# A scan's output projection from f16 halves with a factor per chunk, in another place of the step

## The chip, the cores and the metric

One core of a Trainium2 chip runs the whole program. The metric is device time in microseconds (us). "Before" is the kernel as it stands, "after" the one with the change. The engines are named as the profile does: PE (TensorE matmuls), PEld (its weight loads), DVE (VectorE), ACT (ScalarE), POOL (GpSimd), SP (SyncE, which here only issues DMAs).

## The reference, cut to what matters

```
x   = x + 0.5 * ffn(layernorm(x))            # quantised weight, LoRA, bias; 2048 tokens x 512
n   = layernorm(x)
h   = n' + mamba2(rmsnorm(n))                # residual of the block is the layer-normed input
        zxbcdt = h @ w_in.T                  # z 512, x 128, B 128, C 512, dt 4
        causal convolution with 4 taps, silu; dt = softplus(dt + bias)
        scan over 16 chunks of 128 tokens, 4 heads of 128: Y from att * X and from the state
        y = (Y + D x) * silu(z)              # 2048 x 512
        return y @ w_out.T                   # 512 x 512: the product that is changed
h2  = rmsnorm(h);  mlp = (silu(h2 @ gate.T) * (h2 @ up.T)) @ down.T      # inner size 1792
x   = x + h + mlp
x   = x + 0.5 * ffn(layernorm(x))
```

## The kernel before, in words

Tokens are worked in 16 chunks `c` of 128 and in 4 strips `i` of 512 (`c = 4i + j`). Nearly all large products are made of f16 halves: a value is scaled, ACT writes its f16 rounding ("hi"), DVE the f16 of the rest ("lo"), and the helper `product` (its matmul is L1960) sums hi*hi, hi*lo and lo*hi for each of four 128-row blocks, so 12 matmuls of 512 columns for one product of 128 x 512 x 512. A few products are still in f32; the profile shows each f32 matmul as two records.

The middle of the program is `step(c)` for c = 0 to 15, written once for each engine as a fixed order of work, which is all the order there is: every engine runs its own list and waits on semaphores.

- TensorE's step: `s1(c+1)` (decay rows and transposes of the next chunk), `f(c+8)` (first ffn of a later chunk, while there is one), `s2_diag`, `s2_state`, `s2_inner` (the scan proper; `s2_diag(c)` and `s2_state(c)` sum into the bank `B_YT`), `s1_bc(c+1)`, one `proj` of the next strip (a product, the first of `SLOTS[j]`), with j = 0 also `steps` and with j = 2 `csm`, then `w(c)` (the output projection, L2083: four f32 matmuls of `szs` with `w_out`), then the remaining one or two `proj` of `SLOTS[j][1:]`. In the last strip (c = 12 to 15) two products `gate_up(0, j)` stand in place of the `proj`.
- `steps(i)` makes the four step-size columns of each chunk of a strip with `product`: 48 matmuls of 4 columns. `csm(i)` sums them along the tokens.
- DVE's step: tap sums of the convolution for the late `proj` of the step before (`taps`, L1450, after ACT has copied the bank out with `conv`, L885), `x1_stats(c+8)` (L1382, L1289), `gate_y(c)` (Y times silu(z), L1425, ends the use of `B_YT`), `lo2(c-1)` (the lo half of h2, L1376), `advance(c)` (the state, L1432), `weights` and `scan1(c+1)` (L1415, on which POOL's `scan_d` and then `s2_diag(c+1)` wait), `lo1`, `prep0`, the taps of the first slot, `residual2(c)` (L1441: n1 plus the bank of `w(c)`).
- ACT's step: `scan_ecs`, `scan1`, `conv` and tanh of the late slots, `hi0`, `hi2(c-1)`, `scan_decay(c+1)`, `hi1`, `scan2(c+1)`, `renorm(c)` (n1, L799), `conv` and tanh of the first slot, `square(c)` (sum of squares of the residual, L803).
- POOL's step: the rsqrt and shift of ln1 and ln0, `scan_c`, `scan_d`, the DMA `xb`, `rms2(c)` (from `square(c)`; it then issues the DMA that adds x2 into xs), and in some steps the sums `t_op` for the later Strassen products.
- SP issues the loads of x, the transposes `t0`, `t1(c+8)` and `t2(c-1)` (h2 into `h2`), one queue in order.

Banks of the `proj`, `f` and `w` products are handed out by a list (`PLAN`) that is built in the order of TensorE's step. `w_out` is loaded whole in f32 early on, and its memory later becomes one of the three homes of the gated values. After step 15 come the mlp products and the second ffn, which the change touches only by their first waits.

## Times and profile before

| what | value |
|---|---|
| median of 3 runs | 767.16 us (766.51 to 767.99) |
| the profiled execution, its own time | 768.65 us |
| its span on the core | 766.9 us |
| PE busy | 755.4 us, 98% |
| DVE busy | 626.5 us, 82% |
| ACT busy | 446.4 us, 58% |
| POOL busy | 337.2 us, 44% |
| granted TensorE clock | 9 tenths or more in all 40 slices, 1.00 in every window read |

The page gives the busy time of each engine, then the span in 40 slices, then the chain of work that ended last, then groups of instructions. PE is busy in nearly the whole span, so a time can be found by adding up PE's list, provided that no other engine keeps PE waiting; the waits and the windows say how near the others are to doing so. Matmul durations in the rows overlap each other, so the cost of a group is read from start to start, or in the chain, which counts no overlap.

### The profile page before, as it was taken

The page shows a single profiled execution, that of the slowest core. Times are in us where ns is not written, and L with a number is a line of the kernel's source. Part 1 is how long each engine was busy: PE and PEld are TensorE (multiplying, and loading weights), DVE is VectorE, ACT ScalarE, POOL GpSimd, SP SyncE. Part 2 cuts the span into 40 slices and gives each one's busy share as a digit, 9 for nine tenths or more (in the row PEclk, how much of TensorE's full clock was granted, in tenths as well). Part 3 has the DMA queues.
Part 4 walks back from the last instruction along what each step waited for, and adds up shares of the span by engine and source line. Part 5 has one row for each costly group of instructions (what it writes and reads, how often), then busy time and mean ns, then how long its engine had stood idle before and what let it go on. Part 6 is the DMA issues. An engine that isn't in the chain of part 4 may idle for free.

```text
span 766.9 us, 10654 instructions
## 1 busy us (share of the span) xinstructions
PE 755.4 (98%) x3469; PEld 353.2 (46%) x3470; DVE 626.5 (82%) x1230; ACT 446.4 (58%) x881; POOL 337.2 (44%) x392
## 2 busy tenths in 40 slices
PE   8999999999999999999999999999999999999998
PEld 3444554454555444444443444444444444444443
DVE  6888878878878979878799978878878878767994
ACT  3877767766686766643545556456456456444441
POOL 5631534663442379775413333233233233224574
PEclk9999999999999999999999999999999999999999
DMA  8843543552321211420521743743743743443565
GB/s 311 171 75 71 139 94 83 110 111 60 78 56 28 42 38 42 114 55 1 124 47 23 172 77 64 163 77 62 164 77 65 162 77 66 79 77 69 119 169 138
DMA packets 95414, 71.86 MB, mean 94 GB/s; under 512 B 65232, under 2 KB 72400, under 8 KB 95360
## 3 DMA queue, kind: packets, MB, share of 16 engines
q0 software_dynamic: 17280, 31.46, 23.0%
q1 hardware_dynamic: 77600, 39.66, 19.5%
q8 instruction: 28, 0.46, 0.2%
q14 instruction: 26, 0.21, 0.1%
q10 hardware_dynamic: 480, 0.07, 0.1%
HBM read 20.32 MB, written 4.19 MB: 32 GB/s over the span
## 4 chain that ended last, share of the span: by engine, by line
PE 77%; DVE 13%; ACT 4%; issue 3%; POOL 2%; DMA 1%; ACTq 0%; POOLq 0%; DVEq 0%
PE PS L1960 64%; PE PS L2083 4%; PE PS L2183 3%; DVE raw L1450 2%; PE PS L2091 1%; DVE stage L1450 1%; PE PS L2056 1%; DVE state L1432 1%; PE PS L2065 1%; DVE st L1289 1%; PE PS L2073 1%; PE PS L2048 1%; DVE xs L1382 1%; DVE S L1415 1%; DMA h<-lora_b_t 1%
## 5 line engine op out<-in xcount | busy, mean ns | idle before, releaser
L712 POOL DMA_DIRECT2D xs<-x x59 | 50.9, 864 | 151.2 <-ACT x L1159 137.1
L1960 PE MATMUL PS<-h,w_in 128*128 128x512 f16 x480 | 108.7, 379 | 0.2 <-issue 0.2
L1960 PE MATMUL PS<-h,x_t 128*128 128x512 f16 x408 | 94.0, 379 | 0.0
L1960 PEld LDWEIGHTS PS<-h,w_in 128*128 128x128 f16 x480 | 46.9, 98 | 65.3 <-issue 15.5
L1960 PE MATMUL PS<-n_T,stage 128*128 128x512 f16 x288 | 71.5, 379 | 0.0
L1159 ACT ACTIVATE x<-PS,d_d 128x512 f32<-128x512 f32 x59 | 40.2, 682 | 39.1 <-PE PS L1960 39.1
L1960 PEld LDWEIGHTS PS<-h,x_t 128*128 128x128 f16 x408 | 39.5, 98 | 48.5 <-issue 2.3
L521 POOL TENSOR_TENSOR r<-mv,mhalf 128x1 f32<-128x1 f32 (+1 forms) x32 | 29.4, 917 | 72.2 <-DVE mv L1293 55.0
L712 POOL DMA_DIRECT2D xs<-n x29 | 25.2, 868 | 71.1 <-ACT n L1159 60.8
L1960 PE MATMUL PS<-pre,stage 128*128 128x512 f16 x192 | 49.3, 379 | 0.0
L1129 ACT ACTIVATE xds<-tm,dgh 128x512 f32<-128x512 f32 x24 | 17.3, 722 | 53.0 <-DVE tm L1889 53.0
L1960 PEld LDWEIGHTS PS<-n_T,stage 128*128 128x128 f16 x288 | 28.1, 98 | 34.0 <-ACT x L1159 0.3
L1960 PE MATMUL PS<-w_ffn,raw_gu 128*128 128x512 f16 x192 | 43.2, 379 | 0.0
L1450 DVE SCALAR_TENSOR_TENSOR raw<-pre,cw,raw 128x512 f32<-128x512 f32 x36 | 28.0, 777 | 10.4 <-ACT raw L885 10.1
L1960 PE MATMUL PS<-raw,x_t 128*128 128x512 f16 x144 | 34.7, 379 | 0.4 <-DVE Ld L1842 0.4
L1960 PE MATMUL PS<-w_in,x_t 128*128 128x512 f16 x144 | 34.8, 379 | 0.0
L1159 ACT ACTIVATE n<-PS,d_d 128x512 f32<-128x512 f32 x29 | 19.8, 683 | 23.8 <-PE PS L1960 22.5
L1960 PE MATMUL PS<-h,n 128*128 128x512 f16 x144 | 33.2, 379 | 0.3 <-DVE n L1530 0.3
L2083 PE MATMUL PS<-w_out,stage 128*128 128x512 f32 x64 | 29.3, 600 | 0.3 <-DVE stage L1425 0.2
L1960 PEld LDWEIGHTS PS<-pre,stage 128*128 128x128 f16 x192 | 18.7, 98 | 22.7 <-ACT x L1159 0.3
L1960 PEld LDWEIGHTS PS<-w_ffn,raw_gu 128*128 128x128 f16 x192 | 18.7, 98 | 22.7 <-DMA raw_gu<-h2n_p 0.3
L2083 PE MATMUL PS<-w_out,raw 128*128 128x512 f32 x64 | 29.0, 595 | 0.1
(314 smaller groups left out, 1819.3 us busy)
## 6 DMA issues: line engine op xcount, KB each, us to landing
xs<-x POOLq DMA_DIRECT2D x75, 256.0 KB, 3.3
xs<-n POOLq DMA_DIRECT2D x29, 256.0 KB, 3.3
x_t<-x_in SPq DMA_DIRECT2D x16, 256.0 KB, 3.0
x_t<-hb POOLq DMA_DIRECT2D x16, 256.0 KB, 3.8
out<-x_t SPq DMA_DIRECT2D x16, 256.0 KB, 2.3
raw_gu<-gate_t SPq DMA_DIRECT2D x7, 512.0 KB, 4.4
raw_gu<-up_t SPq DMA_DIRECT2D x7, 512.0 KB, 6.6
raw_d<-down_t SPq DMA_DIRECT2D x7, 512.0 KB, 7.3
```

Source lines behind the costliest of these rows:

```text
L521: return po.tensor_tensor(dst, src, mhalf[:, 0:src.shape[-1]], ALU.pow)
L712: po.dma_start(chunk_of(xs, c), d_tmps[d % 3], accum_op=ALU.add).then_inc(s_acc[d % 3], 16)
L1129: ac.activation(th_s[ab], u4 if ab else c11, ACT.Tanh, scale=dgh[:, p % 2:p % 2 + 1]).then_inc(e_tanh_g, 1)
L1159: ac.activation(d_tmps[d % 3], bank(d_bank(d)), ACT.Copy, scale=d_d[:, p % 3:p % 3 + 1]).then_inc(e_ev, 1)
L1289: link(ve.bn_stats(stat, src), e_link, base + 1)
L1382: link(ve.scalar_tensor_tensor(chunk_of(xs, c), bank(b), 0.5 / ACT_SCALE if c < NF else d_f[:, :], x_t[:, j, :], ALU.mult, ALU.add), e_x1, ...
L1415: last = ve.scalar_tensor_tensor(S[:, s, h, :], heads(B_G)[:, h, :], dt[:, (c // CH) % 2, j * H + h:j * H + h + 1], Ld[:, h, :], ALU.mult, ...
L1432: last = ve.scalar_tensor_tensor(state[:, h, :], state[:, h, :], ecs[:, s, h, P - 1:P], heads(B_SS)[:, h, :], ALU.mult, ALU.add)
L1450: ins = ve.scalar_tensor_tensor(xbc[i % 2][:, b, :], pre[:, w, k:k + ST], cw[:, b, k:k + 1], xbc[i % 2][:, b, :], ALU.mult, ALU.add)
L1960: ins = pe.matmul(out_, lhs(a, b, k), rhs(a, b, k), start=first and n == 0, stop=last and n == len(todo) - 1)
L2083: last = pe.matmul(bank(b), y[:, h, (c % CH) * P:(c % CH + 1) * P], w_out[:, h, :], start=h == 0, stop=h == H - 1)
L2183: last = pe.matmul(bank(B_P[c % 2]), nT32[c % 2][:, k, :], wf[:, k, :], start=k == 0, stop=k == KB - 1)
```

## The change

- `w(c)` becomes a `product`: 12 f16 matmuls instead of four f32 ones. `w_out` is cut once, in the prologue, into f16 halves with a power-of-two scale per row (`wo_sum`, `wo_hi` on ACT, `wo_scale`, `wo_lo` on DVE). Its f32 load goes to a part of `h2` that held the quantised weight (`wo_raw`), is issued after the small loads and waits for the ffn weight (`e_wf`).
- y is cut in every chunk, with a factor for the chunk: ACT sums its squares (`y_sum`), TensorE adds them over the partitions with one f32 matmul of one column into `B_YT` (`y_over`), DVE takes it with a floor (`y_max`), POOL takes the powers -1/2 and 1/2 (`y_scale`), ACT writes hi (`y_hi`), DVE lo (`y_lo`). `residual2` multiplies the bank with the factor back.
- `w(c-1)` stands in step c, ahead of the first `proj`, and `w(15)` after `gate_up(0, 4)` in the bank `B_CS`. With it `residual2`, `renorm`, `square` go from c to c-1, and `hi2`, `lo2`, `rms2`, `t2` from c-1 to c-2 (`rms2` to the head of POOL's step). `csm` stands ahead of the `proj`, `bound_turn(0)` behind `s1_bc`. Four `t_op` of c = 14 go behind the last step, around `rms2(15)`.
- `s2_diag(c)` waits for `y_max(c-1)` instead of `gate_y(c-1)`.
- `steps` uses hi and lo weights side by side in eight columns (`w_dt`): 32 matmuls instead of 48, one small DVE add more.
- Several one-off semaphores give way to the engines' own counters (same waits).

```diff
-        w_out = sb("w_out", [P, H, DM])
+        w_out = sb("w_out", [P, 2, H, DM], F16)
-            sp_.dma_start(w_out[:, :, :], w_out_t...).then_inc(s_wout, 16)
+            sp_.wait_ge(e_wf, KB)
+            sp_.dma_start(wo_raw, w_out_t...).then_inc(s_wout, 16)
...
+            def y_scale(c):
+                po.wait_ge(e_ym, c + 2)
+                po.tensor_tensor(y_s[:, c, :], y_m[:, c, :], halves[:, :], ALU.pow).then_inc(e_yscale, 1)
...
             def step(c):                     # POOL
+                if c > 1:
+                    rms2(c - 2, c % CH)
                 ...
                     scan_d(c + 1, (c + 1) % CH)
+                y_scale(c)
...
+            def y_sum(c):
+                ac.wait_ge(e_y, c + 1)
+                ac.activation(junk..., y_of(c), ACT.Square, accum_out=ssy[:, c:c + 1]).then_inc(e_ysum, 1)
+            def y_hi(c):
+                ac.wait_ge(e_yscale, c + 1)
+                if c > 0:
+                    ac.wait_ge(e_wo, c)
+                ac.activation(y_hl[:, 0, :, :], y_of(c), ACT.Copy, scale=y_s[:, c, 0:1]).then_inc(e_yhi, 1)
...
+            def y_max(c):
+                ve.wait_ge(e_yall, c + 1)
+                ve.tensor_scalar(y_m[:, c, :], PS[:, B_YT, 0:1].broadcast_to([P, 2]), Y_TINY, None, ALU.max).then_inc(e_ym, 1)
+            def y_lo(c):
+                ve.wait_ge(e_yhi, c + 2)
+                ve.scalar_tensor_tensor(y_hl[:, 1, :, :], szs[(c // CH) % 2][:, :, cols], y_s[:, c, 0:1], y_hl[:, 0, :, :],
+                                        ALU.mult, ALU.subtract).then_inc(e_ylo, 1)
...
-                ve.tensor_tensor(x2[:, j % 2, :], n1[:, :], bank(PLAN["w", c][0]), ALU.add).then_inc(e_x2, 1)
+                ve.scalar_tensor_tensor(x2[:, j % 2, :], bank(PLAN["w", c][0]), y_s[:, c, 1:2], n1[:, :], ALU.mult, ALU.add)...
...
             def w(c):
-                for h in range(H):
-                    last = pe.matmul(bank(b), y[:, h, ...], w_out[:, h, :], start=h == 0, stop=h == H - 1)
+                pe.wait_ge(e_ylo, H + c + 1)
+                pe.wait_ge(*freed)
+                product(bank(b), lambda a, b, h: y_hl[:, a, h, :], lambda a, b, h: w_out[:, b, h, :], H).then_inc(e_wo, 1)
+            def y_over(c):
+                pe.wait_ge(e_ysum, c + 2)
                 pe.wait_ge(e_y, c + 1)
+                pe.matmul(PS[:, B_YT, 0:1], ssy[:, c:c + 1].broadcast_to([P, P]), over[:, :], start=True, stop=True).then_inc(e_yall, 1)
...
             def s2_diag(c, j):
-                    pe.wait_ge(e_y, c)
+                    pe.wait_ge(e_ym, c + 1)
...
             def step(c):                     # TensorE
                 ...
                     s1_bc(c + 1)
+                if c > 0:
+                    w(c - 1)
+                if j == 2 and i + 1 < NS:
+                    csm(i + 1)
                 if i + 1 < NS:
                     proj(i + 1, SLOTS[j][0])
                     if j == 0:
                         steps(i + 1)
                 else:
                     gate_up(0, j)
-                w(c)
                 if i + 1 < NS:
-                    for q in SLOTS[j][1:]:
+                    for n, q in enumerate(SLOTS[j][1:]):
                         proj(i + 1, q)
+                        if n == 0:
+                            y_over(c)
...
             gate_up(0, EARLY_GU)
+            w(NCH - 1)
             bound_spread(1)
```

In the last strip `y_over(c)` stands between the two products of `gate_up(0, j)`.

## Rows read from the trace of the kernel before

**Rows 1.** Page, part 1: busy us, share of the span, instructions.

```profile
PE 755.4 (98%) x3469; PEld 353.2 (46%) x3470; DVE 626.5 (82%) x1230; ACT 446.4 (58%) x881; POOL 337.2 (44%) x392
```

**Rows 2.** Waits of PE, whole span: waiting line <- line waited for: us, times, longest.

```profile
PE PS L2056 <- POOL S L555: 1.0, 1, 1.0
```

**Rows 3.** Windows, from s1 to s1: length, busy (count) PE, PEld, DVE, ACT, POOL, clock, DMA.

```profile
106.40:174.60 68.20, 67.93 (x334) 33.87 (x333) 56.52 (x140) 49.16 (x111) 35.71 (x44) 1.00 0.42 88
174.60:240.00 65.40, 65.24 (x321) 32.67 (x320) 53.33 (x123) 47.90 (x113) 27.21 (x34) 1.00 0.29 60
240.00:296.40 56.40, 54.57 (x229) 26.97 (x227) 47.39 (x108) 39.48 (x93) 30.97 (x31) 1.00 0.19 38
296.40:338.30 41.90, 41.88 (x174) 20.35 (x172) 37.47 (x60) 21.50 (x48) 33.17 (x32) 1.00 0.35 82
```

**Rows 4.** Chain that ended last, in order of time: start, us, what.

```profile
97.83 3.54 PE PS L2083 x8
...
122.42 0.70 DVE raw L1450
...
227.70 3.78 PE PS L1960 x60
...
305.66 3.43 PE PS L2083 x8
...
390.17 2.59 PE PS L1960 x12
392.76 0.31 PE PS L2129 x2
```

**Rows 5.** Timeline of PE about 121 and 199 us: start, us, instructions.

```profile
121.88 0.39 PE L2037 MATMUL PS<-cs_b,sel_b 80*128 80x128 bf16 x4
...
130.98 0.29 PE L2012 MATMUL PS<-dA,tri 128*128 128x16 f32 x2
131.12 0.42 PE L2013 MATMUL PS<-tri,dA 128*80 128x128 f32 x2
```

**Rows 6.** Timelines of DVE and (the L549 row) POOL: start, us, instructions.

```profile
119.24 0.68 DVE L1364 TENSOR_TENSOR hn_p<-hn,hn_p 128x512 f16<-128x512 f32 x1
...
133.20 0.74 DVE L1376 SCALAR_TENSOR_TENSOR h2n_p<-x,r,h2n_p 128x512 f16<-128x512 f32 x1
...
340.51 0.15 DVE L1497 COPY mxa<-PS 128x3 f32<-128x3 f32 x1
...
115.62 1.56 DVE L1376 SCALAR_TENSOR_TENSOR h2n_p<-x,r,h2n_p 128x512 f16<-128x512 f32 x1
...
115.36 1.27 POOL L549 TENSOR_TENSOR stage<-stage,ecs 128x512 f32<-128x512 f32 x1
```

**Rows 7.** Waits of DVE, 106.4 to 174.6 us.

```profile
DVE raw L1450 <- ACT raw L885: 3.1, 3, 1.3
DVE stage L1450 <- ACT stage L885: 2.8, 2, 2.0
```

**Rows 8.** Timeline of ACT in the prologue; in brackets the idle time before.

```profile
21.39 1.26 ACT L1017 ACTIVATE stage<-raw 128x1284 bf16<-128x1284 f32 x1
...
45.38 0.20 ACT L864 ACTIVATE pre<-hist 128x3 f32<-128x3 f32 x1 [3.11 <-PE PS L1960]
...
70.34 0.20 ACT L883 ACTIVATE pre<-hist 128x3 f32<-128x3 f32 x1 [3.57 <-PE PS L1960]
```

**Rows 9.** DMA issues with us to landing, then the DVE read of the fifth x chunk.

```profile
w_out<-w_out_t SPq DMA_DIRECT2D x1, 1024.0 KB, 12.5
...
27.64 0.69 DVE L1289 BATCH_NORM_STATS2 st<-x_t 128x6 f32<-128x512 f32 x1
```

**Rows 10.** Timelines of DVE, POOL and PE about 306 to 310 us.

```profile
305.89 1.11 DVE L1415 SCALAR_TENSOR_TENSOR S<-PS,dt,Ld 128x128 f32<-128x128 f32 x4
...
308.25 1.27 POOL L555 TENSOR_TENSOR S<-S,d_diag 128x512 f32<-128x512 f32 x1
...
309.57 1.12 PE L2056 MATMUL PS<-S,tm 128*128 128x512 f32 x2
```

240 lines of the change are left out of this document (150 added, 90 removed).

## The prediction

> **What bounds the kernel now.** I read the page's busy times first. PE is busy in 98% of the span, DVE in 82% [rows 1], so the first guess is that the end is set by the sum of PE's list. The waits of PE bear that out: after the first 100 us the longest is 1.0 us, once [rows 2]. But an average hides stages, so next I cut the scan into windows from one `s1` to another [rows 3]: steps 1 to 4, 5 to 8, 9 to 12, and 13 to 15 with the product behind them. PE fills all of them (67.93 of 68.20 us, 65.24 of 65.40, 54.57 of 56.40, 41.88 of 41.90). DVE is busy 56.52, 53.33, 47.39 and 37.47 us in them, 82 to 89%. That is little room for an engine that takes its work in a fixed order and gets it from ACT: in the first window 5.9 us of its idle time are waits for ACT's copies of `proj` banks [rows 7]. The chain confirms how near the two are. For long stretches it runs through DVE and ACT, not through PE (one link is shown in [rows 4]), and comes back to PE where PE waited no more than 1.0 us. So PE bounds, and a loop of DVE and ACT is about as long in steps 1 to 3 and 5 to 7. I expect a saving on PE to be paid out in part only.
>
> **The projection.** The chain gives `w` 3.54 us where f16 work follows and 3.43 otherwise [rows 4]; of the 16, seven are of the long kind, mean 3.48. A product of 12 f16 matmuls is 2.59 in the same view [rows 4]. Saving 0.89 x 16 = 14.2 us (13.4 to 15.2 by either row alone).
>
> **Step sizes.** A `proj` with `steps` behind it is 3.78 us for 60 matmuls [rows 4]; less 2.59, the 48 small ones cost 1.19, or 0.025 each. Eight columns instead of four should cost the same, as the weight load sets this pace; 16 fewer save 0.40, four times: 1.6 us. DVE gets one more small operation each time.
>
> **`y_over`.** No such matmul exists before: f32, weights of 128 x 128 by broadcast, one column, two passes, between two f16 products. Two rows are near. The f32 pair of `csm` with 16 columns takes 0.14 from its start to the next [rows 5], but a further f32 load follows it; the f32 pair of `bound_spread` with 3 columns between f16 products takes 0.31 in the chain [rows 4]. I take 0.31, as its neighbours are the same, and 0.14 to 0.41 as ends (0.1 for a load that is not hidden): 5.0 us for 16, 2.2 to 6.6.
>
> **PE in sum.** -14.2 - 1.6 + 5.0 = -10.8 us, with ends -14.6 and -8.4. Each of the first three windows gets some 2.7 us shorter for PE.
>
> **What DVE gets.** `y_max` is a tiny read of a bank, like the 0.15 us copy [rows 6]. `y_lo` is an operation like `lo2`, 0.74, of which the next can hide 0.08 [rows 6]; `residual2` grows by some 0.06. That is 0.9 us for each step, 3.5 for four. DVE would be busy 60.0 of 65.5 us in the first window (92%), 56.8 of 62.7, 50.9 of 53.7, and 40.2 of 40.2 in the last, where three steps and a bit remain. ACT gets `y_sum` and `y_hi`, 0.7 and 0.6; it has 19 us of idle time in the first window and is no bound by itself, but it stands between DVE's pieces. I went through steps 1 to 4 with the durations of the timeline. In step 1 `square(c-1)` now stands ahead of `scan2`, so ACT must wait for `residual2(c-1)`, which costs the `conv` of the first slot some 1.9 us. Against that `renorm` and the old `square` are out of ACT's way between two `conv`, and `y_hi` lies under DVE's taps: two DVE waits of the [rows 7] kind, 0.65 and 1.3 us, mostly go. The loop of four steps comes to some 65 to 66 us, against 65.5 for PE. I take 0.7 us of PE waits in each of the first three windows.
>
> **The last steps.** `scan1(14)` ends at 307.0, POOL's `scan_d` at 309.5, and `s2_diag(14)` starts at 309.57 [rows 10]: here the three engines are already level, and DVE gets later by 0.9 a step. Half of the waits for `hi2` go, since `lo2` is a step later. I take 1.0 us lost. `w(15)` and all behind it (`square`, `rms2`, `hi2`, `lo2`, `t2`) stand behind one more `gate_up`; the product that needs them, `gate_up(0, 6)`, has `gate_up(0, 5)` and a `down`, about 10.5 us, ahead of it, and the tail adds up to some 8 to 9. Nothing taken, up to 1.5 if that cover is gone.
>
> **New waits and moved steps.** `s2_diag` waits for `y_max`, and on PE all later work is queued behind it. Between `y_over(c)` and `s2_diag(c+1)` PE has `s1` and either `f` or one more product, 3.0 us, but in steps 9 and 11 only `s1`, 0.45; I take 0.3 for these two together. `csm` comes 9.1 us after the step's start, as before (121.88 to 130.98 [rows 5]), because `w` and the `proj` have changed places. `y_scale` holds POOL's `xb` by about 1 us, with 9 us before that chunk is read. On SP, `t2` a step later lets the transposes of the other kinds go ahead.
>
> **The prologue.** `wo_sum` and `wo_hi` are 2048 elements; by the 1.26 us for 1284 they take 2 us each, and they fall where ACT was idle for 3.11 and 3.57 us for PE [rows 8]. `wo_scale`, the `w_dt` copies and four `wo_lo` give DVE 4.5 us in 64; most fall into gaps of 0.7 to 0.9. The load of `w_out`, 1 MB, took 12.5 us to land [rows 9]. It now starts when the ffn weight is done, near 18.5 us, so it shares the DMA engines with the next x chunks, whose first is read by DVE at 27.64 [rows 9], about 1 us after it lands. I take 0.3 us for all of this, 0 to 3.
>
> **Result.** -10.8 + 3 x 0.7 + 1.0 + 0.3 + 0.3 = -7.1 us, against which the 1.8 us that PE stood idle in the third window [rows 3] is half POOL's `t_op` ahead of `scan_d`; with `rms2` no longer waiting there for ACT some 0.6 of it should go: -7.7. The profiled execution took 768.65, 1.5 more than the median and 1.75 more than its span; the same parts give 761.0 for it and 759.5 for the median. The forecast's own range is 756.5 to 763.
>
> **A rule of the skill, weighed.** The trace shows one DVE form with two durations: `lo2` 0.74 us, and 1.56 when it starts 0.26 us after POOL's 1.27 us tensor operation [rows 6]. The Trainium skill, in "SBUF — State Buffer", section "SBUF: two separate sides", says that VectorE and GpSimd share a pair of ports as an exclusive lock, and that a VectorE operation with two SBUF inputs is held for the whole of a GpSimd operation that reads SBUF. By that rule, the trace agrees, and `y_lo`, which reads both y and its hi half from SBUF, is open to it where `residual2`, with one input from PSUM, was less so. It is the mechanism of the second rival.
>
> **The rivals.**
>
> 1. *No stall.* DVE's gaps take all the new work and PE is never held: -10.8 with the idle time of the third window recovered by 0.6, 756. For it: PE idles 0.3 and 0.2 us in the first two windows. Against: the loop's length above.
> 2. *The loop takes over.* Each `y_lo` meets a POOL operation and takes 1.56 instead of 0.74, 3.3 us more in a window. DVE would be busy 63.3 of 65.5 us, more than it has ever managed here, so the windows stay as long as they are, and only the `steps` of the prologue and `w(15)` save, 0.4 + 0.9 = 1.3 us: 765.9, with 763 to 768 as its width. Against: POOL is idle where `y_lo` falls, after the taps of the first slot.
> 3. *The ring (slower).* The factor of a chunk goes from TensorE to DVE and back within one step, and DVE reaches `y_max` only after `scan1`, `residual2` and `lo1`. DVE's `lo1` ended at 119.9 us in step 1 [rows 6], and PE would be done with `y_over` 14.3 us after the step's start at 106.4, at 120.7: DVE is 0.8 us early. In the last steps it comes within 0.3 us of being late. If DVE is late by W in each of 15 steps, PE stands still W each time. It decides from W = 10.8 / 15 = 0.72 us. With one held operation (0.82) and the 0.2 of a handover W is 1.02, and the time 767.2 - 10.8 + 15.3 = 772.
> 4. *It does not do what it says.* `y_over` costs the upper end, and the halves a start of their own at each product: -6, of which the same 3 are lost: 764.
>
> **How the numbers follow.** Forecast 0.48, no stall 0.13, the loop 0.20, the ring 0.15, the last 0.04. A measurement of this kernel can tell about 0.2%, 1.5 us, from no change. Faster by more: 0.48 + 0.13 + half of the loop + 0.03 = 0.74. Within: 0.09. Slower: the ring and the slowest of the loop, 0.17. The range 755 to 768 leaves out the ring and the lower ends of the costs with no stall, together 0.19.
>
> **What would show each step.** L-rows of the new `w`: 2.59 us in the chain, 16 times; `y_over` 0.31 from start to start; `steps` 0.8 behind its `proj`. The windows of steps 1 to 4, 5 to 8 and 9 to 12 at 66.2, 63.4 and 53.8 us with DVE over 90%; waits of PE on DVE or POOL of some 3 us in sum, at `s2_diag` above all. `y_lo` at 0.74 and not 1.56. The prediction is wrong if `s2_diag` waits on `y_max` in most steps, if PE's start of the scan comes later by more than 1 us (the x load), or if DVE still has 3 us of waits for `conv` in a window.

## The result, and the profile after

The changed kernel takes 794.41 us (median of 4 runs, 792.89 to 795.70) against 767.58 before (766.51 to 769.62). The ratio is 1.0352, with a 95% interval of 1.0336 to 1.0369. The forecast of 759.5 us is 35 us off and has the wrong sign. The profiled execution took 793.92 us, with a span of 792.2 (before: 768.65 and 766.9).

First the busy times of the changed kernel's page:

```profile
PE 750.3 (95%) x3502; PEld 352.3 (44%) x3502; DVE 646.5 (82%) x1277; ACT 470.6 (59%) x932; POOL 354.2 (45%) x411
```

PE is now idle for 41.9 us, where before it was 11.5 [rows 1]. That is the first thing to see: PE's list was to get shorter and did, as shown below, but PE stands still more often. The next view says where. These are the windows of steps 1 to 4, 5 to 8, 9 to 12, and 13 to 15 with the product behind them, as [rows 3] has them of before. The columns are stretch, length, busy us (count) of PE, PEld, DVE, ACT and POOL, granted clock, DMA share, GB/s:

```profile
100.90:170.46 69.56, 64.81 (x341) 33.17 (x340) 59.01 (x148) 53.87 (x122) 38.34 (x46) 1.00 0.40 80
170.46:238.58 68.12, 62.67 (x329) 31.88 (x328) 57.06 (x134) 53.04 (x125) 33.09 (x43) 1.00 0.35 63
238.58:306.06 67.48, 55.61 (x252) 27.64 (x251) 51.71 (x119) 42.74 (x102) 32.19 (x33) 0.95 0.16 32
306.06:362.60 56.54, 47.38 (x206) 23.68 (x204) 43.33 (x73) 31.18 (x70) 32.51 (x33) 0.91 0.29 66
```

Before, they were 68.20, 65.40, 56.40 and 41.90 us long. So the first step starts 5.5 us earlier (100.90, not 106.4: part of it is the row product of chunk 0, which now comes later), and then +1.4, +2.7, +11.1 and +14.6 are lost; behind the scan +1.0. That sums to the 25.3 us between the two spans. Of the 30.8 us lost behind the start of step 1, 25.7 lie in the last two windows, seven steps and a product. These are differences to before; the forecast had the first two windows 2.0 us shorter each, so they miss it as well. The idle time of PE in the four windows (length less busy) is 4.8, 5.5, 11.9 and 9.2 us, where before it was 0.3, 0.2, 1.8 and 0.0. In the last two windows the granted clock is below 1.00 as well.

PE's waits from 84 to 365 us (waiting line <- line waited for: us in total, times, longest):

```profile
PE PS L2151 <- DVE y_m L1482: 7.0, 2, 4.2
PE PS L2107 <- DVE dA L1694: 4.3, 3, 2.3
PE PS L2126 <- DVE sp L1659: 3.6, 3, 1.3
PE PS L2053 <- DVE x L1524: 3.3, 2, 1.7
...
PE PS L2053 <- DVE mxa L1580: 1.8, 1, 1.8
```

No single one is the answer. PE waits for `y_max` twice, for `dA` (in `csm`), for the bank that `residual2` frees, for a small read of a bound. Before, the longest wait here was 1.0 us, once [rows 2]. A wide spread of small waits, nearly all for DVE (two for POOL's S come to 2.2 us, one for ACT's `y_sum` to 1.6), suggests that DVE is late as a whole; so the next rows are waits of DVE (first two) and ACT (the next two) in the same stretch, and under them ACT's wait for `residual2` in the kernel before:

```profile
DVE y_m L1482 <- PE PS L2179: 16.7, 8, 3.1
...
DVE h2n_p L1437 <- ACT h2n_p L812: 7.2, 4, 3.9
...
ACT junk L822 <- DVE x L1524: 19.9, 13, 2.6
...
ACT y_hl L837 <- POOL y_s L570: 10.6, 9, 2.2
```

```profile
ACT junk L803 <- DVE x L1441: 6.2, 7, 2.0
```

DVE waits 16.7 us for `y_over` (L2179), with everything it has to do queued behind `y_max`. ACT waits 19.9 us for `residual2`, 13 times, where before it was 6.2 us in 7: that is `square(c-1)` (L822), which the change has put ahead of `scan2(c+1)`. These two became the suspects.

### The profile page after: what moved, and what is told of

Read it like the earlier page. It is cut to its first block, busy times and chain, and to the rows that moved or that the text cites. A ratio compares the mean times of both kernels' runs of the same rounds, so it can differ in the third digit from the quotient of the medians.

```text
span 792.2 us, 10900 instructions
## 1 busy us (share of the span) xinstructions
PE 750.3 (95%) x3502; PEld 352.3 (44%) x3502; DVE 646.5 (82%) x1277; ACT 470.6 (59%) x932; POOL 354.2 (45%) x411
## 3 DMA queue, kind: packets, MB, share of 16 engines
q1 hardware_dynamic: 77600, 39.66, 19.6%
## 4 chain that ended last, share of the span: by engine, by line
PE 64%; DVE 20%; ACT 6%; issue 4%; POOL 3%; DMA 3%; SPq 0%; ACTq 0%; DVEq 0%; POOLq 0%
PE PS L2053 57%; DVE raw L1533 3%; DVE stage L1533 2%; PE PS L2186 1%; DMA raw_d<-down_t 1%; DVE state L1515 1%; DVE S L1476 1%; PE PS L2151 1%; PE PS L2143 1%; PE PS L2279 1%; PE PS L2160 1%; DVE st L1346 1%; PE PS L2168 1%; ACT xds L877 1%; DVE x L1524 1%
## 5 line engine op out<-in xcount | busy, mean ns | idle before, releaser
L534 POOL TENSOR_TENSOR r<-mv,mhalf 128x1 f32<-128x1 f32 (+1 forms) x32 | 29.9, 935 | 72.6 <-DVE mv L1350 59.0
L1183 ACT ACTIVATE xds<-tm,dgh 128x512 f32<-128x512 f32 x24 | 17.3, 722 | 54.2 <-DVE tm L1979 54.2
L2053 PE MATMUL PS<-w_out,y_hl 128*128 128x512 f16 x192 | 44.8, 384 | 0.1
L2053 PEld LDWEIGHTS PS<-w_out,y_hl 128*128 128x128 f16 x192 | 19.0, 99 | 28.9 <-issue 8.4
```

Of the source, the lines that this page charges most:

```text
L534: return po.tensor_tensor(dst, src, mhalf[:, 0:src.shape[-1]], ALU.pow)
L1183: ac.activation(th_s[ab], u4 if ab else c11, ACT.Tanh, scale=dgh[:, p % 2:p % 2 + 1]).then_inc(e_tanh_g, 1)
L2053: ins = pe.matmul(out_, lhs(a, b, k), rhs(a, b, k), start=first and n == 0, stop=last and n == len(todo) - 1)
```

## The experiments

**How the runs are read.** The starts of `s2_diag` in PE's timeline cut each span into four stages: chunk 0 to 8, 8 to 12, 12 to 15, and the rest. For each kernel I set against them what PE's own list would take, worked out from e2_columns (before's order, with no wait of PE over 1.0 us: 132.8, 60.2, 37.6 and 445.2 us): each row product 3.48 or 2.59 us, `y_over` 0.14 where it exists, and in the new order one row product moved from the first stage to the rest. The difference is the *loss*. Times are medians of four executions (ten for e2_columns and e18_open_no_low); the ratio is to the kernel before, measured beside each, with its 95% interval. Two kernels whose intervals overlap are not told apart here. The times of the stages come from one traced execution of each. "f" marks the fixed factor (no sum of squares, no maximum, no power).

| kernel | time us | ratio | loss 0-8 | 8-12 | 12-15 | rest |
|---|---|---|---|---|---|---|
| changed kernel | 794.41 | 1.0352 [1.0336, 1.0369] | 10.9 | 11.8 | 12.0 | 5.2 |
| e2_columns | 766.02 | 0.9993 [0.9983, 1.0003] | 0 | 0 | 0 | 0 |
| e3_order (f, f32) | 784.87 | 1.0229 [1.0212, 1.0247] | 1.1 | 4.3 | 8.0 | 4.6 |
| e1_no_ring (f) | 782.31 | 1.0202 [1.0175, 1.0230] | 6.0 | 7.9 | 9.7 | 7.6 |
| e4_over_earlier | 785.88 | 1.0245 [1.0228, 1.0262] | 6.4 | 7.6 | 11.8 | 4.7 |
| e5_csm_back (f) | 783.83 | 1.0220 [1.0205, 1.0235] | 7.4 | 7.8 | 9.5 | 7.2 |
| e6_last_strip (f) | 778.15 | 1.0151 [1.0134, 1.0168] | 5.8 | 7.9 | 9.1 | 3.2 |
| e7_places_back (f) | 779.74 | 1.0167 [1.0152, 1.0182] | 6.5 | 9.2 | 8.5 | 3.4 |
| e8_halves_old_order (f) | 804.12 | 1.0484 [1.0469, 1.0500] | 29.9 | 10.0 | 8.3 | 2.8 |
| e9_rms2_first (f) | 778.10 | 1.0150 [1.0133, 1.0166] | 5.9 | 10.2 | 8.4 | 3.3 |
| e10_no_low_pass (f) | 778.75 | 1.0155 [1.0129, 1.0181] | 5.8 | 8.4 | 7.7 | 3.0 |
| e11_extra_passes | 778.95 | 1.0154 [1.0139, 1.0169] | 4.0 | 5.1 | 2.0 | 1.4 |
| e12_ring_mended | 785.39 | 1.0245 [1.0209, 1.0281] | 7.6 | 8.6 | 7.2 | 9.2 |
| e13_square_back (f) | 774.27 | 1.0084 [1.0061, 1.0107] | 3.9 | 5.3 | 7.0 | 5.2 |
| e14_square_strip (f) | 774.82 | 1.0088 [1.0064, 1.0112] | 3.8 | 6.8 | 7.4 | 4.8 |
| e15_ring_square | 782.25 | 1.0186 [1.0157, 1.0215] | 5.9 | 7.5 | 9.4 | 5.4 |
| e16_loop_mended (f) | 775.96 | 1.0115 [1.0096, 1.0133] | 5.6 | 6.0 | 7.3 | 3.1 |
| e17_passes_off_chain | 772.33 | 1.0077 [1.0060, 1.0094] | 0.1 | 0.8 | 3.8 | 1.6 |
| e18_open_no_low (f) | 770.33 | 1.0043 [1.0028, 1.0058] | 3.9 | 6.1 | 4.8 | 3.2 |

### First the three parts of the change, one by one

**e1_no_ring.** The changed kernel without the factor's ring.

```diff
-                po.wait_ge(e_ym, c + 2)
-                po.tensor_tensor(y_s[:, c, :], y_m[:, c, :], halves[:, :], ALU.pow).then_inc(e_yscale, 1)
+            chain(po.memset(y_s[:, :, 0:1], 2.0 ** 8))
+            chain(po.memset(y_s[:, :, 1:2], 2.0 ** -8))
```

(`y_sum`, `y_over` and `y_max` return at once; `y_hi` and `s2_diag` wait for `gate_y`.)

> The kernel after without the factor per chunk: no sum of squares of y (y_sum), no y_over, y_max or y_scale; y is cut with a fixed factor, and s2_diag waits for gate_y again. The halves, the order and the eight columns stay. In the kernel after, DVE waits 16.7 us for y_over at y_max, and PE 7.0 us for y_max. Theory A (the way of the factor from TensorE to DVE and back within one step is the cause): most of the 27 us goes, 762 us or less. Theory B (the order is the cause: the sum of squares of the residual ahead of scan2, residual2 behind scan1, csm ahead of the row product): at most 10 us come back, 784 to 790 us.

**e2_columns.** Before, with eight-column step sizes.

```diff
+                    for k in range(KB):
+                        pe.matmul(PS[:, B_TB, at:at + 2 * H], h2T[0][:, k, tokens], w_dt[:, k, :], start=k == 0, stop=False)
```

> The kernel before with the eight-column step sizes alone. PE does 0.4 us less in each of four places, DVE one small operation more on the path to the transposes of the next strip. If PE alone bounds: 766.0 us (1.6 less). If the longer start of the softplus holds PE where the kernel after shows a wait of 1.2 us on it, three times: 767 to 770.

**e3_order.** e1_no_ring with before's projection in it: `w(c-1)` stands where the change has it, but multiplies y and the weight in f32.

```diff
-                product(bank(b), lambda a, b, h: y_hl[:, a, h, :], lambda a, b, h: w_out[:, b, h, :], H).then_inc(e_wo, 1)
+                for h in range(H):
+                    last = pe.matmul(bank(b), y[:, h, (c % CH) * P:(c % CH + 1) * P], w_out[:, h, :], start=h == 0, stop=h == H - 1)
```

> The kernel after with the projection in f32 as before, no halves and no factor: what remains is the order (w, residual2, square, renorm one step later, hi2, lo2, rms2, t2 two steps, csm ahead of the row product) and the eight columns. Theory A: the order is harmless, 766 us. Theory B: it costs by itself, 780 us and more, with PE waiting for residual2 (a bank) and for dA.

**e4_over_earlier.** The changed kernel with `y_over(c)` behind the first projection of the step, not the second, in chunks 0 to 11.

```diff
                     proj(i + 1, SLOTS[j][0])
                     if j == 0:
                         steps(i + 1)
+                    y_over(c)
```

> The kernel after with y_over one product earlier in steps 0 to 11 (behind the first row product instead of the second). In steps 0, 4 and 8, DVE waits 3.0 us for it at y_max and PE 1.2 us for the softplus that stands behind; both should go. Theory A: 3 x 3 us on DVE, of which PE gets back 4 to 8 us, 786 to 790. Theory B: no more than 2 us, as DVE then waits for ACT instead.

What was measured: from 766.02 (columns) the order alone goes to 784.87, +18.9 us; the halves in that order to 782.31, -2.6 where the list says -14.2; the ring to 794.41, +12.1, of which 8.5 go when `y_over` stands one product earlier. So no part does what the forecast gave it except, within the noise, the columns (-1.0 us against the kernel before beside it), and the largest item is the new order, with not one instruction more than before on PE: for all waits of the change together the forecast had 3 x 0.7 + 1.0 + 0.3 = 3.4 us. The steps add up to the result by the way they are taken: 766.0 + 18.9 - 2.6 + 12.1 = 794.4. The -2.6 is hardly more than noise, as the intervals of e1_no_ring and e3_order overlap.

By their own theories: e2_columns came out at the time for PE alone (766.0), e3_order as theory B (780 and more). e1_no_ring gave back 12.1 us, between theory A (762 or less) and B (at most 10 back), nearer to B. e4_over_earlier gained a little more than its theory A (786 to 790). One thing differs between e2_columns and e3_order beside the order: the one-off semaphores that became counters. e17_passes_off_chain below has the counters in before's order and takes the steps of e2_columns up to chunk 12, so they are not the cause up to there.

### What of the order costs: places that made no difference

**e5_csm_back, e6_last_strip, e7_places_back, e9_rms2_first** each start from e1_no_ring (e7 and e9 from e6).

```diff
e5:  +                    if j == 2:
     +                        csm(i + 1)              # behind proj(i + 1, SLOTS[j][0])
e6:  +                if c >= 3 * CH:
     +                    y_hi(c)                     # ACT, ahead of square and scan2
     +                if c >= 3 * CH:
     +                    y_lo(c)                     # DVE, ahead of t_los and gate_up
e7:  e5, e6, scale_read(0) ahead of lo2, and
     +                if j == 2:
     +                    residual2(c - 1, (c - 1) % CH)   # ahead of scan1(c + 1)
e9:  e6, and on POOL
     +                if c >= 2 * CH + 2:
     +                    rms2(c - 1, (c - 1) % CH)   # ahead of sums(c)
```

> This is the kernel of e1_no_ring (fixed factor 2^8, so that the sum of squares, its row product, y_max and the power are left out; the rest is the whole computation) with one edit: the decay products csm(i + 1) of chunks 2, 6 and 10 stand behind the first of the three projections again, not ahead of it. e1_no_ring took 782.31 us. Its three long steps (from one s2_diag to the next) were those of chunks 2, 6 and 10: 19.6, 21.1 and 21.3 us, where before with the eight columns has 18.1, 18.1 and 16.1 for a row product that is 0.9 us dearer: 11.5 us over. PE's waits for dA in them add up to 4.0 us. Theory A, the place of csm costs: behind the projection dA has been ready for 0 to 2 us, the 4.0 us go and most of what they drag along, 775 to 778 us. Rival B, in these steps DVE and ACT bound, and csm's wait only shows it: a wait of the same length comes up behind it (for the S of POOL, or for the bank that residual2 frees), 781 to 783 us.

> The kernel of e1_no_ring (fixed factor, as said there) with one edit, for chunks 12 to 15 alone: y_hi stands ahead of square and scan2 on ACT, and y_lo right behind scan1 and residual2 on DVE, ahead of the four differences t_los and of gate_up. In e1_no_ring the row product of chunk 12 waits 4.5 us for y_lo, which stands behind t_los (0.68, 0.68, 1.65, 1.63 us) and gate_up on DVE, while chunk 13's two gate_up products, which wait for nothing, stand behind it on PE. Theory A, this queueing costs the last strip most of its loss (steps of 13.2, 13.7, 18.5 and 12.4 us against 14.3, 12.6, 12.8, 12.2, and 454.5 behind it against 445.2): the 4.5 us, and 2 to 3 us of half clock behind them, go, 774 to 777 us. Rival B, the wait moves to POOL's S of chunk 14, which is due at the same time (t_op of 1.3 to 1.7 us each stand ahead of it): 780 to 782 us.

> The kernel of e1_no_ring (fixed factor, as said there) with four places changed: csm as in e5_csm_back, the last strip as in e6_last_strip, the read of the bounds scale_read(0) of chunk 10 ahead of lo2 again (the third product of that step waits 1.8 us for the bank that it frees), and residual2 ahead of scan1 in chunks 2, 6, 10 and 14 (a third projection waits 4.2 us in sum for the bank it frees). Theory A, the order loses at these places and nowhere else: 782.3 - 4 - 2.6 - 1.8 - 4.2 - 6.5 gives 763 us, 760 to 768, below before's 767. Rival B, DVE and ACT bound the loop whatever the places (the halves cost each of them one pass more a chunk), and what is mended at one place comes back at the next: 773 us or more.

> The kernel of e6_last_strip (778.15 us; fixed factor, so no sum of squares, maximum or power) with POOL's rms2(c - 1) ahead of the sums t_op of step c from chunk 10 on, where it stands behind them, at the head of step c + 1; and hi2 and lo2 of chunk 10 behind the decay, as from chunk 11 on. In e7_places_back four t_op (1.7, 1.6, 1.2, 1.3 us) stand ahead of rms2, ACT's hi2 waits for it with scan_decay queued behind it, and DVE's lo2 waits 3.8 us with advance, weights and scan1 of chunk 13 behind it; S of chunk 13 then comes 1.5 us late for PE and that of chunk 14 4.7 us late. Theory A, this queue on POOL is what the last strip still loses: 772 to 775 us. Rival B, DVE is busy without a gap from 298 to 314 us of that trace, so the wait only moves: 777 to 779 us.

Only e6 moved anything: -4.2 us against e1, nearly all of it behind chunk 15, a result between its two theories (774 to 777, and 780 to 782). The row on which it rests, from the timelines of e1_no_ring (DVE, then PE; start, us, what, and in brackets the idle time before and its releaser):

```profile
296.71 0.69 DVE L1640 TENSOR_TENSOR w_in<-hn,w_in 128x512 f16<-128x512 f32 x1 [2.48 <-ACT w_in L1171]
297.32 0.68 DVE L1640 TENSOR_TENSOR w_in<-h2n,w_in 128x512 f16<-128x512 f32 x1
297.92 1.65 DVE L1640 TENSOR_TENSOR w_in<-n_p,w_in 128x512 f16<-128x512 f32 x1
299.49 1.63 DVE L1640 TENSOR_TENSOR w_in<-hn_p,w_in 128x512 f16<-128x512 f32 x1
...
302.36 1.55 DVE L1489 SCALAR_TENSOR_TENSOR y_hl<-raw,y_s,y_hl 128x512 f16<-128x512 f32 x1
...
303.97 4.45 PE L2055 MATMUL PS<-w_out,y_hl 128*128 128x512 f16 x12 [4.54 <-DVE y_hl L1489]
```

PE's row product of chunk 12 is released by `y_lo`, which DVE reaches after `t_los` and the gate of a product that does not need it. The other three went as their rival B, and none is told apart from its base (+1.5 us, +1.6 us and 0). In e5 csm's wait for `dA` (4.0 us) is gone, and the waits behind it grow: for the bank of `residual2` from 4.2 to 5.6 us in sum, for the bound (`mxa`) from 1.8 to 4.4; the stage stays as long. e7 shortens the step of chunk 10 from 21.3 to 18.4 us and lengthens that of chunk 11 from 13.2 to 17.4; e9 shifts loss in the same way. A wait that comes back elsewhere when it is mended was not what set the time.

### The closed chain

**e10_no_low_pass** takes the suspected load off DVE, **e11_extra_passes** puts it where before has none, **e8_halves_old_order** tries the halves without the shift by a chunk.

```diff
e10: -                ve.scalar_tensor_tensor(y_hl[:, 1, :, :], ..., y_hl[:, 0, :, :], ALU.mult, ALU.subtract).then_inc(e_ylo, 1)
     +                ve.tensor_copy(y_hl[:, 1, 0, 0:1], ...).then_inc(e_ylo, 1)
e11: +                y_hi(c)                     # ACT, behind scan2(c + 1), ahead of renorm(c) and conv
     +                    y_lo(c)                     # DVE, ahead of residual2(c)
e8:  -                    w(c - 1)                    # ahead of the projections of step c
     +                    w(c)                        # behind them
```

> Halves without the new order: before with eight columns for the steps, the projection from f16 halves with a fixed factor 2^8 for y (no sum of squares, no maximum, no power), and the row product w(c) still in its own step, but behind all projections of that step (in the last strip where before has it); residual2, square, hi2, lo2, POOL's rms2 and csm stand as in before's order, so that all of them still come in the step of their chunk or right behind it. Theory A, the halves gain what PE's list says and the order of the change loses: 766.0 - 14 = 752 us, 751 to 757. Rival B, the halves cannot be had, whatever the order, as DVE and ACT have one pass more a chunk (0.74 and 0.71 us) and already run nearly as long as PE: 762 to 768 us.

> The kernel of e9_rms2_first with the pass y_lo cut to one element a partition: the low half of y stays zero, so the output is not the reference's, while PE's twelve matmuls, all waits and all places are the same. It takes 16 passes of 0.74 us (up to 1.75) off DVE. DVE is busy 62.4 of the 70 us from 90 on in e1_no_ring, against 57.3 before. Theory A, DVE is the bound of the loop once the product is short: PE gets back 6 to 12 us against e9_rms2_first. Rival B, it is the hand-overs in queue order (ACT waits for DVE, DVE for ACT) and not the load: 0 to 3 us.

> The other way round: before with the eight-column steps, its row product in f32 in before's place and everything in before's order, plus the two passes of the halves, whose results nobody reads: ACT's copy of y to f16 behind scan2 (0.71 us) and DVE's difference ahead of residual2 (0.74 us), once a chunk. PE's list is that of e2_columns, 766.02 us. Theory A, before's order has room for them (DVE idle 12.7 of 70 us in its loop, all of it hidden by PE's 3.5 us product): 766 to 768.5 us. Rival B, before's loop is at its limit already, and each pass comes out at the end: 772 to 778 us.

These three runs moved the suspicion from load to place. e8, at 804 us, lies outside both of its theories (751 to 757, 762 to 768): PE waits 17.3 us in sum for `y_lo` of its own chunk up to 345 us, and 12.8 and 5.1 us for the banks that DVE and ACT free, so halves without the shift by a chunk lose more than halves with it. In e10 16 passes of DVE are gone and nothing comes back that can be told apart (778.10 to 778.75). The Trainium skill, in "Perfetto Trace Analysis", section "Optimization Strategies", says of such a picture that one should optimize the engines that keep the matmul engine waiting. Here taking load off DVE gave nothing (this run), while moving one pass on ACT gave 8.0 us (e13 below). In e11 the same 16 passes, with one on ACT each, cost 12.9 us, 0.8 a chunk and just above its rival B (772 to 778), in a kernel where PE is the bound and DVE was idle 11.5 us of the 70 from 90 us on. Load alone can't explain both. Place can: one row each of e2_columns and e11_extra_passes (DVE's first taps of step 0's slot), and under them what stands ahead on ACT in e11:

```profile
96.89 2.33 DVE L1455 SCALAR_TENSOR_TENSOR raw<-pre,cw,raw 128x512 f32<-128x512 f32 x3 [0.67 <-ACT raw L886]
```

```profile
97.89 2.33 DVE L1530 SCALAR_TENSOR_TENSOR raw<-pre,cw,raw 128x512 f32<-128x512 f32 x3 [1.27 <-ACT raw L928]
...
95.21 0.70 ACT L835 ACTIVATE y_hl<-stage,y_s 128x512 f16<-128x512 f32 x1
95.82 0.80 ACT L815 ACTIVATE n<-xs,b,r 128x512 f32<-128x512 f32 x1
```

The scan starts 0.4 us later in e11; the other 0.6 of the 1.0 us is ACT's pass, which delays the convolution that DVE is already waiting for. ACT and DVE hand each slot to and fro: conv, taps, tanh, silu, then the next slot. Here a pass ahead of the hand-over lengthens that chain by its whole duration. In this step PE does not pay for it (18.6 us in both kernels); in the steps of chunks 2 and 6, with three slots, it does: 19.7 and 19.5 us for 18.1.

**e17_passes_off_chain** is the test: the same passes, ACT's where it waits for the taps, DVE's where it waits for the next convolution.

```diff
                     slot_a(i + 1, SLOTS[j][0])
+                    y_hi(c)                     # ACT: behind conv, ahead of tanh
                     slot_b(i + 1, SLOTS[j][0])
...
+                y_lo(c)                         # DVE: last in the step
```

> e11_extra_passes (778.95 us: before's order and f32 row product, eight-column steps, plus two passes a chunk that nobody reads) with the two passes moved: ACT's behind the convolution of the slot, where it fills ACT's wait for the taps (2.2 us), and DVE's at the end of the step, behind silu, where DVE waits for the next convolution (0.6 to 1.8 us); in e11_extra_passes they stood ahead of the convolution and ahead of residual2 and silu. As many passes, as long, as in e11_extra_passes. Theory A, a pass costs by its place in the chain of hand-overs conv, taps, tanh, silu: 766 to 769 us. Rival B, a pass costs as such, 0.4 us of each: 775 us or more.

The time, 772.33 us, lies between the two theories, and the stages say why. To chunk 12 the steps are those of e2_columns to within 0.9 us in 193, with 12 more passes on each engine's list: 8.2 of e11's 9.1 us are gone, with every pass still there, so up to chunk 12 the place is the price. Of the 6.3 us that remain, 5.4 lie behind chunk 12, where e11 itself lost 3.4: there the new places are worse, not better. Three of its `y_lo` from chunk 10 on take 2.15, 2.62 and 1.64 us and not 0.75, where POOL's tensor operations run; in e11 it is one, at 1.55.

**e13_square_back, e14_square_strip, e15_ring_square** undo the one such place that the new order has made.

```diff
-                if c > 0:
-                    square(c - 1, (c - 1) % CH)
                 if c + 1 < NCH:
                     scan2(c + 1, (c + 1) % CH)
...
+                if c > 0:
+                    square(c - 1, (c - 1) % CH)      # behind slot_b and sp_exp
                 if i + 1 < NS:
                     slot_a(i + 1, SLOTS[j][1])
```

> The kernel of e1_no_ring (782.31 us; fixed factor, so no sum of squares, maximum or power) with one edit: square(c - 1) stands on ACT behind the slot of its step, as before, and no longer ahead of scan2(c + 1). In the traces of the new order ACT waits there for residual2(c - 1), which DVE runs last of a series, 1.6 to 2 us a chunk, and scan2 and the convolution stand behind: with square itself the convolution starts 2.5 us later than its inputs allow, and the next taps, tanh and silu follow one upon the other. Theory A, this closed loop sets the step where the product no longer does: 1.5 to 2 us for chunks 2, 6, 10, 12 and 13 and some half clock, 770 to 775 us. Rival B, DVE's own series is full in those steps (no gap from 120.8 to 136.4 us in e10_no_low_pass), and what comes earlier from ACT waits for DVE: 779 us or more.

> e6_last_strip (778.15 us; fixed factor, as said there) with square(c - 1) behind the slot as in e13_square_back. Theory A: the two add up, 766 to 770 us. Rival B, a full DVE: 775 us or more.

> The whole computation with the factor per chunk: e4_over_earlier (785.88 us) with square(c - 1) behind the slot. Theory A: the same gain as without the ring, 774 to 778 us. Rival B: 783 us or more. A third reading, by e4_over_earlier's own trace: y_over waits for y_sum on ACT 9.0 us in sum (7 times, up to 2.7 us), and this y_sum comes no earlier by the edit, so that only half of A's gain shows: 780 us.

e13 gives back 8.0 us of 782.3, the most of any move within the order, as its theory A had it. Step 1 of the changed kernel shows the chain that it cuts (DVE, ACT, DVE):

```profile
115.37 0.74 DVE L1524 SCALAR_TENSOR_TENSOR x<-PS,y_s,n 128x512 f32<-128x512 f32 x1
...
116.14 0.63 ACT L822 ACTIVATE junk<-x 128x512 bf16<-128x512 f32 x1 [1.00 <-DVE x L1524]
116.68 0.19 ACT L822 ACTIVATION_READ_ACCUMULATOR junk<-x 128x1 f32 x1
116.77 1.26 ACT L877 ACTIVATE xds<-tm,wv 128x128 f32<-128x128 f32 x4
...
118.51 0.76 ACT L928 ACTIVATE raw<-PS,cb,cw 128x512 f32<-128x512 f32 x1
...
119.30 0.75 DVE L1533 SCALAR_TENSOR_TENSOR raw<-pre,cw,raw 128x512 f32<-128x512 f32 x1 [1.29 <-ACT raw L928]
```

`residual2` is the last of DVE's series advance, weights, `scan1`; `square` waits for it; `scan2`, whose inputs had been ready since `weights` (L1467, 114.41), is behind; then the convolution, and DVE's taps wait for that. So each step's DVE series must end before the next one's taps can begin: a closed loop through two engines. In e13_square_back the same step has no wait on ACT (ACT, then DVE), and the last row is the first of these taps in its base, e1_no_ring:

```profile
112.05 1.28 ACT L878 ACTIVATE xds<-tm,wv 128x128 f32<-128x128 f32 x4
...
113.81 0.76 ACT L929 ACTIVATE raw<-PS,cb,cw 128x512 f32<-128x512 f32 x1
...
115.24 0.75 DVE L1535 SCALAR_TENSOR_TENSOR raw<-pre,cw,raw 128x512 f32<-128x512 f32 x1
```

```profile
116.83 0.75 DVE L1535 SCALAR_TENSOR_TENSOR raw<-pre,cw,raw 128x512 f32<-128x512 f32 x1 [1.59 <-ACT raw L929]
```

The taps come 1.6 us earlier. Step 1 itself takes PE 14.28 us with or without the move; the steps of chunks 2, 6 and 10 go from 19.6, 21.1 and 21.3 to 18.5, 20.0 and 19.7 us, and by stage the move takes 2.1, 2.6, 2.7 and 2.4 us off the loss. What it would give with the f32 product, in e3_order, where the order costs its 18.9 us, was not run; ACT waits 31.3 us for `residual2` there and 32.0 in e1_no_ring.

e14 shows that the gains of e6 and e13 do not add (774.82, where 766 to 770 was expected): against e13 it loses 1.5 us more in chunks 8 to 12. With the ring in (e15) the move gives 3.6 us, about half of what it gave in e13, as the third reading had it, though 782.25 us lies between that reading's 780 and rival B's 783. So with `y_over` and `square` both moved the ring still costs 8.0 us (782.25 against 774.27).

### What is still lost

**e12_ring_mended** is e4_over_earlier with e9's POOL order and `y_max`, `y_lo`, `y_hi` early in the last strip; **e16_loop_mended** is e13 with `csm` back, `residual2` ahead of lo2, and the decay's passes ahead of `lo1`; **e18_open_no_low** is e13 without the low pass.

```diff
e12: +                if c >= 3 * CH:
     +                    y_max(c)
     +                    lo2(c - 2)
     +                    y_lo(c)
e16: +                if j == 2:
     +                    residual2(c - 1, (c - 1) % CH)   # ahead of lo2 and advance
     +                if j == 2 and i + 1 < NS:
     +                    cut_decay(i + 1, 0)              # ahead of lo1
     +                    cut_decay(i + 1, 1)
e18: e13, and y_lo as in e10
```

> The whole computation with the factor per chunk, as in the changed kernel, but with y_over one product earlier (as in e4_over_earlier, 785.88 us), rms2 ahead of the sums (as in e9_rms2_first), and for chunks 12 to 15 y_max ahead of lo2 and of t_los and bounds, y_lo right behind lo2, and y_hi ahead of t_his and the gate's tanh. In e4_over_earlier y_max waits behind t_los and bounds twice, 4.2 and 2.8 us of PE time, and the row product of chunk 12 behind y_lo. Theory A, the loss of the last strip is this queueing on DVE, POOL and ACT: 785.9 - 7 - 5 gives 774, 771 to 777 us. Rival B, y_max, a DVE pass that waits for a PE product in the middle of the queue, holds DVE up for as long as it gains: 782 us or more.

> The kernel of e13_square_back (774.27 us; fixed factor, so no sum of squares, maximum or power) with four places changed in the steps of chunks 2, 6 and 10: csm behind the first projection; residual2 ahead of lo2 and advance on DVE (the third projection waits 1.0 to 1.8 us for the bank that it frees); the five passes of the decay's column product (cut_decay) ahead of lo1 and of the statistics of x; scale_read ahead of both. Theory A, places: with the bank and cs_b in time these steps go from 18.5, 20.0 and 19.7 us to 17.3 to 18 us, in all 4 to 5 us: 769 to 771 us. Rival B, DVE is full: in e13_square_back it runs without a gap from 120.2 to 137.1 us, 16.9 us for a step in which PE has 17.2 us of work and hands over twice; mending places only exchanges what is late: 773 us or more.

> The kernel of e13_square_back (774.27 us; fixed factor) with the pass y_lo cut to one element a partition, as in e10_no_low_pass: the low half of y stays zero, so the output is not the reference's; PE's matmuls, all waits and all places are those of e13_square_back. In that kernel 21 us are still lost against PE's own list. Theory A, DVE is full in the steps of chunks 2, 6, 8 to 15: its 0.74 us (1.6 beside POOL's sums) come back there, 8 to 12 us, 762 to 766. Rival B, a further chain of hand-overs sets those steps: under 3 us, 771 us or more, as when the same pass was taken from e9_rms2_first (778.1 to 778.75 us).

e12 takes 4.6 us from chunks 12 to 15 and gives 4.5 back behind them: 785.39 against 785.88, nothing (rival B). e16 gave nothing either (775.96 against 774.27, rival B): PE's waits for `dA` go from 2.8 us to none and those for the bank from 3.0 to 1.2, and new ones come for `cs_b` (3.6 us) and the bound (3.6 us). In step 2, which stays at 18.5 us, the new one is this:

```profile
133.31 0.40 PE L2136 MATMUL PS<-cs_b,sel_b 80*128 80x128 bf16 x4 [1.05 <-DVE cs_b L1463]
```

e18 took 3.9 us off e13 (774.27 to 770.33). Its gain stands in the last strip and behind it (losses of 4.8 and 3.2 us for 7.0 and 5.2); up to chunk 8 the steps are the same to 0.1 us. So neither theory of e18 (762 to 766, and 771 or more) holds as written. From chunk 12 on, where DVE's series has no gap (298 to 314 us in e7_places_back), its load does count. In steps 2 and 6, 18.5 and 20.0 us against 17.2 of PE's work, it does not, and it is open what sets them. One possibility is argued only: the start of DVE's long series at 120.2 us of e13 is released by a convolution on ACT, which is itself behind the tanh that waited for the taps before, so a further chain of hand-overs is likely. No kernel tried beats e2_columns, and of the 21 us that e13 and the 28 us that e15 lose against PE's list most have no shown cause.

## Why the prediction was wrong

**What bounds.** Right for before, and the warning was in the text: "a loop of DVE and ACT is about as long". It was then weighed by busy shares and by one walk through steps 1 to 4. e11 and e17 show that share alone does not tell: the same passes cost 12.9 or 6.3 us, and up to chunk 12 9.1 or 0.9.

**The projection.** Right by its rows: 2.59 us from start to start, as below. **`y_over`.** The rows gave 0.14 and 0.31, I took 0.31; it is 0.13 to 0.15 in 12 of 16 steps, 0.24 in two, and in two a wait follows it. **Step sizes.** The small matmuls of the first `steps` take 0.80 us in place of 1.21 in the traces, as forecast; in the time e2 shows 1.0 us of the 1.6, no more than can be told apart from nothing.

```profile
108.76 2.75 PE L2053 MATMUL PS<-w_out,y_hl 128*128 128x512 f16 x12
111.35 5.34 PE L2053 MATMUL PS<-h,w_in 128*128 128x512 f16 x24
116.53 0.28 PE L2179 MATMUL PS<-over,ssy 128*128 128x1 f32 x2
116.67 0.38 PE L2132 MATMUL PS<-cs_b,sel_b 80*128 80x128 bf16 x4
```

So PE's list is shorter by more than forecast, 13.6 us (14.2 + 1.6 - 2.2, with `y_over` at 0.14), and this term decides nothing.

**What DVE gets: the step that failed.** The forecast saw that "`square(c-1)` now stands ahead of `scan2`, so ACT must wait for `residual2(c-1)`", priced it at 1.9 us in one step, and set it off against two other waits that "mostly go", from one walk through four steps. Then it took 0.7 us of PE waits a window. Those windows came out at 69.56, 68.12 and 67.48 us, not 66.2, 63.4 and 53.8. Undoing that place alone gives 8.0 us (e13). With the ring in, it gives 3.6 us (e15). The error is not the 1.9 us (the taps of step 1 come 1.6 us earlier in e13), and the two waits did shrink: in the first window DVE waits 2.1 us for ACT's convolution, not 5.9 [rows 7]:

```profile
DVE raw L1533 <- ACT raw L928: 2.1, 3, 1.3
```

The error is the set-off and the 0.7 us drawn from it: PE stood idle 4.8, 5.5 and 11.9 us in these windows all the same. That waits in the middle of a chain are no credit against a link that closes it is my reading of this; no run separates the two. And the sum treated step 1 as a sample of all; up to chunk 12 the loss is mostly in the steps of chunks 2, 6 and 10, with three slots each, where the loop is longest (in e1_no_ring 19.6, 21.1 and 21.3 us, in e2_columns 18.1, 18.1 and 16.1 with the dearer product).

**The last steps.** "I take 1.0 us lost": the last window came out 14.6 us longer, the largest single miss. Its list on PE is nearly unchanged, as four row products at 2.59 us stand in it for three at 3.48. Its text had the fact that mattered, "here the three engines are already level", and priced only the added durations. What the traces show is queue order: `y_lo` and `y_max` behind `t_los`, `bounds` and the gate (e1's rows above; moving `y_lo` gives back 4.2 us in e6, moving `y_max` too gives nothing in e12), and POOL's S late in turn. The rest of the 14.6 stays open. From the changed kernel's last strip (PE: start, us, what):

```profile
306.29 0.39 PE L2126 MATMUL PS<-ident,raw 128*128 128x128 f32 x2
310.85 2.04 PE L2151 MATMUL PS<-S,tm 128*128 128x512 f32 x2 [4.18 <-DVE y_m L1482]
312.69 1.91 PE L2160 MATMUL PS<-raw,state 128*128 128x128 f32 x8
```

**New waits and moved steps.** "I take 0.3 for these two together" for `s2_diag` behind `y_max`: PE waited 7.0 us there, in chunks 13 and 15, not 9 and 11. "`csm` comes 9.1 us after the step's start, as before": true of the place, but `dA` comes later with DVE, and `csm` waited 4.3 us. As e5 shows, that wait is a symptom. What is queued behind DVE's own new wait was not asked, though the third rival had "DVE is 0.8 us early" in step 1: `y_max` waited 3.0 us for `y_over` in each of steps 0, 4, 8 and 10, 16.7 in all, because `y_over` stands behind the second projection, too late for a DVE that is not the late one there. Moving it one product forward gives 8.5 us (e4). The 0.6 us that were to come back in the third window did not: PE waits 1.9 us for POOL's S there, before 1.0.

**The signs.** None of the three signs of being wrong came true: `s2_diag` waits for `y_max` twice in 16 steps, the scan starts earlier, and DVE's waits for the convolution are 2.1, 2.4 and 2.3 us in the first three windows. They watched the waits that the forecast had in its sum. The long waits were two others, DVE's for `y_over`, which it had left out, and ACT's for `residual2`, which it had set off; PE's waits, "some 3 us in sum" by the forecast, came to ten times that (31.2 us of idle time in the four windows).

**The rivals.** The ring was the right name for the second-largest part (12.1 us, forecast 772), but its mechanism was inverted: PE was to wait for DVE in every step; PE waits for `y_max` in two steps, and in eight it is DVE that waits for PE. "The loop takes over" had the right engine and the wrong cause: `y_lo` is 0.74 or 0.75 us in 11 of 16 steps; the order costs 18.9 us even with no `y_lo` at all (e3). It let the windows stay as long as before, and so could lose no more than the gain; they got longer. **The prologue** and the **tail** were no part of it: `s2_diag(0)` starts at 88.6 us against 90.4 (88.5 in e2_columns, so the 1.8 us are not the change's), and the stretch behind the scan is 1.0 us longer.

**The range** ended at 768, from bounds on added durations only. The edit reorders the queues of four engines, and that had no term of its own: 3.4 us stood for all waits, and the order alone costs 18.9 (e3).

## What to carry to other kernels

Where two engines hand work to and fro, price a pass by what waits behind it in its queue, not by the engine's idle share: draw the chain of hand-overs once round the loop for the longest step, and see whether an edit closes it or stands ahead of a hand-over. A moved instruction is a change of its own, to be costed for each queue it crosses; a reordering with no new work cost more here (18.9 us) than the ring did (12.1). And when a mended wait comes back one place further on, stop mending waits and look for the loop.

## What the runs showed of the hardware

An f32 pair with a broadcast 128 x 128 weight and one column costs 0.14 us from start to start between two f16 products, half of the 0.31 us of the three-column pair of [rows 4]:

```profile
98.17 0.28 PE L2179 MATMUL PS<-over,ssy 128*128 128x1 f32 x2
98.31 2.75 PE L2053 MATMUL PS<-h,w_in 128*128 128x512 f16 x12
```

Some of PE's waits were paid twice. From 310 to 315 us, with the end of the 4.18 us wait at 310.85, the granted clock is 0.50, which is the 1.2 GHz level, and the pair of `s2_diag` takes 2.04 us instead of 1.02; in the 5 us behind it is back at 0.92, mostly the 2.4 GHz level:

```profile
310.00:315.00 5.00, 4.15 (x11) 2.88 (x12) 4.70 (x8) 3.71 (x10) 4.06 (x4) 0.50 0.00 0
315.00:320.00 5.00, 5.00 (x19) 2.09 (x18) 5.00 (x6) 1.32 (x3) 4.83 (x5) 0.92 0.11 9
```

The length of the wait before is not all that decides this here. Behind the wait of 1.86 us that ends at 254.75 the same pair takes 2.07 us too, while behind those of 2.35 us (265.30) and 2.11 us (354.47) the clock of the next 5 us is 1.00. As an estimate of the sum: PE was idle 30.4 us longer than before and its list 13.6 us shorter; the 25.3 us of the spans leave 8.5 us for this, and the mean granted clock of 0.989 over the span of 792.2 us comes to 8.7. It is a consequence of the waits, not a cause of its own: e11_extra_passes loses 12.9 us at a granted clock of 1.00.

DVE's operations with two inputs in SBUF can take twice as long beside POOL's tensor operations, as the forecast weighed it for `y_lo`; two rows of e1_no_ring, POOL and DVE:

```profile
269.02 1.60 POOL L674 TENSOR_TENSOR n_p<-h 128x512 f32<-128x512 f16 x1
...
269.53 1.64 DVE L1489 SCALAR_TENSOR_TENSOR y_hl<-stage,y_s,y_hl 128x512 f16<-128x512 f32 x1
```

The DVE operation reads y and its hi half from SBUF and takes 1.64 us, not 0.74. That is what the Trainium skill states in "SBUF — State Buffer", section "SBUF: two separate sides", of the pair of ports that VectorE and GpSimd share as an exclusive lock, and the trace agrees. It comes at a bad place: in e1_no_ring the three taps ahead of `s2_diag` of chunk 3 take 2.31 us, those ahead of chunk 11's 3.98, where POOL's sums run beside them.
